# First attention: the exponential taken per head straight from the scores' banks, with the negative maximum as bias

## What is computed

```python
def _L0_attn_ref(x, W_qkv, W_out):
    D_MODEL, N_HEADS, D_HEAD, WINDOW = 256, 16, 16, 64
    SCALE = 1.0 / math.sqrt(D_HEAD)
    qkv = x @ W_qkv
    ...
    scores = jnp.einsum('bhsd,bhtd->bhst', q, k) * SCALE
    scores = scores + _window_mask(S)[None, None]     # j <= i and j > i - 64
    weights = jax.nn.softmax(scores, axis=-1)
    out = jnp.einsum('bhst,bhtd->bhsd', weights, v)
    ...
    return out @ W_out
x = L0_attn_x
x = x + _L0_attn_ref(_layernorm(x, axis=-1), L0_attn_W_qkv, L0_attn_W_out)
```

## Time and profile before

| | |
|---|---|
| median of 3 executions | 2303.82 us (2302.01 to 2306.51) |
| the profiled execution | 2325.94 us, span 2324.2 us |
| mean granted TensorE clock in it | 0.915 of full speed |
| first attention in it | about 28 to 425 us of the span |
| DVE: maximum L371, subtraction L373 | 128 times each, 87.0 and 88.5 us |
| ACT: exponential L443, copy L450 | 128 times each, 80.7 and 76.6 us |

### The profile page before, as it was taken

One profiled execution on the slowest core, in us unless ns is written; L12 is line 12 of the kernel. 1 busy time (PEld: TensorE's weight loads), 2 busy tenths in 40 slices (PEclk: granted clock), 3 DMA queues, 4 the chain that ended last, 5 costly groups with the idle time before them and its releaser, 6 DMA issues. The chain is left out here.

```text
span 2324.2 us, 48998 instructions
## 1 busy us (share of the span) xinstructions
PE 1967.9 (85%) x18133; PEld 1328.0 (57%) x18133; DVE 1704.7 (73%) x2695; ACT 1216.9 (52%) x2198; POOL 475.0 (20%) x608
## 2 busy tenths in 40 slices
PE   5888888799899999989888899999999999861270
PEld 4666666478799999968777333343343343330150
DVE  6667676667578888846644799999999999657822
ACT  4555555333266666622233288888888888620010
POOL 1010100100122233124343112212212212300054
PEclk9999999799899999989999599999999999875585
DMA  2000000461143333333278897774763701020054
GB/s 92 2 0 0 0 0 0 180 246 57 67 159 110 115 118 113 105 106 112 71 238 267 96 83 64 62 45 43 62 47 41 62 20 38 19 73 0 8 178 140
DMA packets 222808, 188.18 MB, mean 81 GB/s; under 512 B 121532, under 2 KB 201368, under 8 KB 220504
## 3 DMA queue, kind: packets, MB, share of 16 engines
q1 hardware_dynamic: 202872, 146.71, 31.7%
q0 software_dynamic: 18080, 27.17, 4.5%
q10 hardware_dynamic: 1728, 12.58, 1.6%
HBM read 121.37 MB, written 64.75 MB: 80 GB/s over the span
## 5 line engine op out<-in xcount | busy, mean ns | idle before, releaser
L2032 ACT ACTIVATE ga_probT<-banks 128x512 f32<-128x512 f32 x1024 | 557.0, 598 | 154.3 <-PE banks L2092 104.2
L1989 DVE TENSOR_REDUCE ga_nmax<-banks 128x1 fp32r<-128x1024 f32 x512 | 610.5, 1219 | 19.6 <-PE banks L2079 18.3
L2079 PE MATMUL banks<-a_ks,a_qs 48*128 48x512 f32 x1024 | 386.5, 460 | 9.7 <-PEq L77 5.6
L2092 PE MATMUL banks<-a_qs,a_ks 49*128 49x512 f32 x1024 | 379.8, 451 | 2.3 <-ACT ga_probT L2032 2.3
L2109 PE MATMUL banks<-ga_probT,a_v 128*32 128x256 f32 x4096 | 331.1, 396 | 6.4 <-ACT ga_o L2038 6.4
L2079 PEld LDWEIGHTS banks<-a_ks,a_qs 48*128 48x128 f32 x1024 | 156.9, 192 | 221.4 <-DVE ga_nmax L1989 175.5
L1955 POOL DMA_DIRECT2D a_qs<-ga_max_rows x256 | 131.4, 521 | 569.7 <-DVE ga_max_rows L1996 528.6
L1450 PE MATMUL banks<-rb_xT,rb_own_w 128*128 128x256 f32 x1872 | 232.2, 283 | 4.6 <-DVE rb_xT L1316 3.7
L1450 PEld LDWEIGHTS banks<-rb_xT,rb_own_w 128*128 128x128 f32 x1872 | 224.7, 190 | 10.7 <-issue 6.7
L2109 PEld LDWEIGHTS banks<-ga_probT,a_v 128*32 128x32 f32 x4096 | 81.4, 108 | 196.9 <-ACT ga_probT L2032 153.1
L1156 PE MATMUL banks<-m_xnT,sh_w 128*128 128x512 f32 x768 | 184.8, 399 | 6.5 <-DVE sh_w L945 5.3
(11 more groups left out here) (326 smaller groups left out, 3203.5 us busy)
## 6 DMA issues: line engine op xcount, KB each, us to landing
rb_w_f<-in_L_ffn_rw_dram SPq DMA_DIRECT2D x39, 512.0 KB
m_xnT<-xnT_parts ACTq DMA_DIRECT2D x12, 1024.0 KB, 4.9
sorted_out<-rb_yb SPq DMA_DIRECT2D x39, 256.0 KB, 2.1
m_w<-in_L_ffn_rw_dram SPq DMA_DIRECT2D x2, 4096.0 KB, 19.9
values<-pg_v SPq DMA_DIRECT2D x16, 512.0 KB, 3.1
a_v<-values SPq DMA_DIRECT2D x16, 512.0 KB, 8.9
a_qs<-queries_rounded SPq DMA_DIRECT2D x28, 256.0 KB, 8.8
a_ks<-keys_rounded SPq DMA_DIRECT2D x28, 256.0 KB, 9.8
```

The source lines that it names most:

```text
L1989: nc.vector.tensor_reduce(nmax[b % 2][:, at:at + 1], slot[:], axis=AX.X, op=ALU.max, negate=True).then_inc(use_read, 1)
L2032: nc.scalar.activation(probT[k % SETS][2 * h + n][:], b_t[ring_place["weights", w] % RING][:], ACT.Exp, scale=SCALE).then_inc(exp_ready, 1)
L2079: return nc.tensor.matmul(slot[:, HALF * kh:HALF * (kh + 1)], qs[a][rows, n, P * q:P * (q + 1)], ks[a][rows, n, HALF * kh:HALF * (kh + 1)] ...
L2092: nc.tensor.matmul(bank[:], ks[a][rows, 2 * gp + n, P * kt:P * (kt + 1)], qs[a][rows, 2 * gp + n, HALF * hf:HALF * (hf + 1)], start=True, ...
```

## The change

ScalarE reads the scores' bank itself, one exponential of 128 x 128 for each of the four heads, with that head's column of `nmax` as bias. VectorE makes the maximum only; `ex`, its semaphore and the subtraction are gone. SCALE moves from the exponential into `head_rows`, so the scores and the maxima come scaled. ScalarE waits for the maximum (`max_ready`), and the mask matmul of the next pair of units waits for the exponentials (`prob_ready`) in place of the subtraction.

```diff
-        ex = [sb(f"ex{k}", [P, HU, W2]) for k in range(2)]
...
-            link(nc.gpsimd.memset(head_rows[:], 1.0))
+            link(nc.gpsimd.memset(head_rows[:], SCALE))
...
                 nc.vector.tensor_reduce(nmax[k][:], sc, axis=AX.X, op=ALU.max, negate=True).then_inc(max_ready, 1)
-                dve.wait_ge(max_ready, ONE + n + 1)
-                nc.vector.tensor_tensor(ex[k][:], sc, nmax[k][:].unsqueeze(2).broadcast_to([P, HU, W2]),
-                                        ALU.add).then_inc(ex_ready, 1)
...
-                act.wait_ge(ex_ready, ONE + n + 1)
+                act.wait_ge(max_ready, ONE + n + 1)
                 if c > 0 or u >= 2:
                     act.wait_ge(probT_done, ONE + n - 1)
-                nc.scalar.activation(prob[k][:], ex[k][:], ACT.Exp, scale=SCALE).then_inc(prob_ready, 1)
+                for j in range(HU):
+                    last = nc.scalar.activation(prob[k][:, j, :], b_s[k][:, W2 * j:W2 * (j + 1)], ACT.Exp, bias=nmax[k][:, j:j + 1])
+                last.then_inc(prob_ready, 1)
...
                     if c > 0 or u >= 2:
-                        pe.wait_ge(ex_ready, ONE + n + two - 1)
+                        pe.wait_ge(prob_ready, ONE + n + two - 1)
```

More of the change, by code:

```diff
@@ L214, in window_attention @@
             "q_done", "q_ready", "k_done", "k_ready", "v_done", "v_ready")]
-        s_done, max_ready, ex_ready, prob_ready, probT_done, probT_ready, out_done = [sem(n) for n in (
-            "s_done", "max_ready", "ex_ready", "prob_ready", "probT_done", "probT_ready", "out_done")]
+        s_done, max_ready, prob_ready, probT_done, probT_ready, out_done = [sem(n) for n in (
+            "s_done", "max_ready", "prob_ready", "probT_done", "probT_ready", "out_done")]
         oT_ready, rsum_ready, onT_ready, on_ready, y_done, x_ready, stats_ready = [sem(n) for n in (
```

## The result

The changed kernel takes 2356.82 us (median of 4 executions, 2352.11 to 2361.81) against 2304.22 for the kernel before beside it: ratio 1.0223, 95% interval 1.0187 to 1.0259, 53 us slower. The forecast was 2360, with 2321 to 2388 as its range.

The account below looks back on a forecast made before the run. No engine is full, so the order of waits bounds the kernel. Path 25 us plus clock falls 31 us gave 56 us on the median of 2303.8, so 2360 us; the 8-in-10 range was 2321 to 2388.

Parts of the forecast that it names:

- The price of the group: ScalarE's four biased exponentials of a unit: 1.14 us against 0.63 for one now; ends 0.78 (bias free) and 1.57.
- The path, pair by pair: Longer chain of waits in a step's four pairs of units: 1.66 us a step, +25 us over 15 steps.
- x: Pair of units in which TensorE also does output projection and transposes; 6.09 us before, forecast +0.20.
- q: Pair of units in which TensorE also does the q matmuls; 6.10 us before, forecast +0.08.
- k: Pair of units in which TensorE also does the k projection; 5.81 us before, forecast +0.37.
- v: Pair with the v projection, four value copies ahead of its second exponentials; 6.10 us before, forecast +1.01.
- S: Start of the block of score matmuls that serves one pair of units; times within a pair count from it.
- The clock: TensorE's clock halving after the v pair's wait, slowing the x pair: 13 falls of 2.4 us, +31 us.
- Rival 1: The path lengthens but the clock holds: 25 us, 2329 us; chance 0.22.
- Rival 2: Faster, VectorE was what mattered: group near 0.63 us, deciding from about 0.75; -10 us, 2294 us; chance 0.04.
- rival 3: No difference: a group between 0.75 and 0.9 us and no falls of the clock, 2304 us; chance 0.06.
- Rival 4: Worse: two clock falls a step or group near 1.3 us; path 39 to 70, clock up to 50; 2404; chance 0.10.

Follow-up runs that it names:

- a_first: Changed kernel with ScalarE's two steps of a place swapped, a unit's exponentials ahead of the copy of the unit before: 2309.10 us, ratio 1.0037.
- a_fill: Changed kernel with six more mask matmuls per step in TensorE's wait before the second mask matmul: 2332.61 us, ratio 1.0130.
- b_fill: Control: the kernel before the change with six more mask matmuls per step at the same place as in a_fill: 2313.85 us, ratio 1.0021.
- a_one: Changed kernel with one exponential of 128x512 per unit, biased by the maximum over all four heads, in place of four: 2294.92 us, ratio 0.9970.
- b_release: Kernel before the change, with only the mask matmuls' wait moved from the subtraction to the exponential: 2396.81 us, ratio 1.0368.
- b_release_fill: b_release with six more mask matmuls in each of the two long waits of a step: 2330.78 us, ratio 1.0095.
- a_first_v7: Changed kernel with exponentials ahead of the copy on ScalarE, and v matmuls and value copies at place 7 instead of 6: 2287.24 us, ratio 0.9906.
- a_one_first_v7: a_first_v7 with one exponential of 128x512 per unit, biased by one maximum over its four heads: 2266.48 us, ratio 0.9817.
- a_v7: Changed kernel with the v matmuls and four value copies at place 7 of a step instead of 6: 2328.45 us, ratio 1.0107.

## Why the prediction was right

**The price of the group** was 1.14 us, and 1.13 to 1.14 was measured. Working it from a biased row of twice the width and the slope between two plain rows was good to a hundredth; the bound of 0.78 (bias free) was 0.35 too low.

**The path, pair by pair.** Forecast x 6.29, q 6.18, k 6.18, v 7.11; at full clock q 6.14, k 6.12, v 6.98, and the x pair of the step without a fall runs from 113.29 to 119.58, 6.29:

```profile
113.29 1.10 PE L585 MATMUL banks<-wa_kT,wa_q_heads 32*64 32x128 f32 x32
...
119.58 1.10 PE L585 MATMUL banks<-wa_kT,wa_q_heads 32*64 32x128 f32 x32
```

The v term was 0.13 too high: the value copies started 3.21 us after S, not 3.32, since the copy ahead of the exponentials starts at 1.72 in the pairs other than x, and I used the x pair's 1.80 for all. The same 0.08 is in the q and k terms, which were 0.04 and 0.06 too high. Together this is the difference between 1.66 and 1.44 us a step, and between the 25 us forecast and the 20.7 measured (18.7 and 2.0 of the first interval). That it is the copy ahead of the exponentials, as the forecast had it, a_first shows.

**The clock.** 13 falls of 2.4 us were forecast, 31 us. Measured in the middle were 12 falls of 2.7 in the mean, 32.9 us, less the one of 2.2 that was there before: 30.7. The forecast did not take that one off, the number was one too high and the size 0.3 too low; that these misses cancel is luck. The forecast gave the wait before the second mask matmul as 2.0 us; it is 1.88, or 1.32 behind 0.50 without a releaser. Two readings of the kernel before: its fall came 1.5 us after the v pair's wait ended (250.36), not 1 us, and the fall of its last step, which the earlier trace rows stops short of, is in the next stretch:

```profile
408.00:412.00 4.00, 3.08 (x36) 2.31 (x37) 1.33 (x3) 0.63 (x1) 0.00 (x0) 0.60 0.01 4
```

That the falls follow the v pair and land at the x pair is as forecast (the clock reads 1.00 until 224 and 0.52 in the 4 us behind). The number of falls was the weakest step, an argument from one fall in 14 steps and from the last step; a_fill and b_fill are what make it a finding.

**Rivals.** Rival 1 (path without clock) was refuted by the trace and is a_fill's state: 25.5 us steps, 2333, where it had put 2329. Rival 2's state (a group near 0.63) was made by a_one: 2295, where it had put 2294. Its threshold of 0.75 us is not contradicted, since 0.68 us gave steps of 23.7, but the kernel's gain is not clear of noise (ratio up to 1.0005), and the pairs are not as it said (v 6.47, not 6.10). No run has a group between 0.75 and 0.9 us, so rival 3 is untested. Rival 4 has two falls a step and a sum of 2404; b_release has them and 2397, but with some 20 us of path and 66 of clock where the rival had 39 to 70 and up to 50, so the nearness of the sum is chance.

**What I had not separated** is what about the release costs. I called it the move of the banks' release from VectorE to ScalarE, behind copies that wait for TensorE. a_first shows the second half to be the cause: it leaves the release with ScalarE and the four pieces as they are, moves only the copy behind them, and the step is 24.15 again. The move by itself, in b_release_fill, costs 1.3 us in another way (one exponential of 0.63 behind the subtraction, in q and v). The length of the group counts too: one exponential in its old place behind the copy gives 23.7, four pieces 25.5. So the loss of 1.44 us needs both, the copy ahead and the long group, and either mending alone removes it.

## What to carry to other kernels

When a wait is moved from one engine to another, list what stands ahead of the signalling instruction in the new engine's queue (here a copy that itself waits for TensorE, and four copies of another stage), and put the signalling work ahead of it before judging the change: the same edit made the kernel 2.2% slower, and 0.9% faster with two changes of order between. A wait that grows on TensorE can be paid twice, as itself and as half clock in the work behind it, and harmless matmuls in the wait tell the two apart, with the same matmuls in the kernel before as a control (where the wait was too short for them they lengthened the step). Before cutting an activation in pieces for a bias per head, look whether the algebra allows one bias for all.

## What the runs showed that I had not expected

**A kernel can get faster by useless matmuls.** 90 repeated mask matmuls in a_fill took 24 us off.

**Every second step of the faster kernels is 0.7 us longer.** In a_first_v7 the steps alternate between 23.52 and 24.2 us, in a_one_first_v7 between 22.1 and 22.9. The loop holds two steps, and PE shows the difference at its back edge, ahead of the next masks:

```profile
242.43 0.60 PE L578 MATMUL banks<-wa_mask,wa_ident_bf 128*128 x2 [0.63 <-issue]
```

0.63 us of idle time that no wait explains ("issue"). The kernel before has the same idle time there (0.66 us at 201.50 of its timeline), but its next mask matmul waits for VectorE anyway. b_fill and a_v7 have it too (0.57 and 0.71 us), and their steps alternate in the same way. That the loop's back edge is the cause is read from the place alone; removing it was not tried.

**The kernel before spreads by chip and execution**: medians of 2304 to 2310, single ones from 2294 to 2319 and the profiled one at 2326, as wide as several of these effects. Whether falls of the clock elsewhere make that spread is open.
